# Residual tokens of x loaded in the steady slots of a perceiver block, into the place of the turned outputs

## The reference

```python
x = x + xattn(layernorm(x), ctx)      # softmax(q k^T / 8) v, heads joined, @ Wo + bo
x = x + attn(layernorm(x))            # note: attn adds its own (normalised) input too
x = x + ffn(layernorm(x))             # relu(x @ w1.T + b1), rounded, @ w2.T + b2, rounded
```

## Time and profile before

| what | us |
|---|---|
| median of 3 runs | 953.22 (950.82 to 953.23) |
| profiled execution | 953.45, span 951.7 |
| PE busy | 928.4 (98% of the span) |
| ACT, DVE, POOL busy | 584.0, 545.4, 493.5 |

### The profile page before, as it was taken

The page is one execution under the profiler, slowest core; times in us unless marked ns, Lnnn a source line. Parts: engine busy times, 40 slices in busy tenths (PEclk is TensorE's granted clock), DMA queues, the critical chain, the costliest instruction groups (busy, mean ns, idle before and its releaser), DMA issues.

```text
span 951.7 us, 19392 instructions
## 1 busy us (share of the span) xinstructions
PE 928.4 (98%) x7405; PEld 577.3 (61%) x7408; DVE 545.4 (57%) x980; ACT 584.0 (61%) x1095; POOL 493.5 (52%) x379
## 2 busy tenths in 40 slices
PE   5999999999999999999999999999999899999998
PEld 3556666666666666666666666666665445444443
DVE  7546555565556655565556655557667625375533
ACT  4577777777777777777777777777774122122220
POOL 3356665655666665655666665657778651110000
PEclk9999999999999999999999999999999899999999
DMA  8266677865766767676767667779978121212312
GB/s 298 67 169 133 132 135 153 147 145 124 143 137 131 139 138 157 137 145 131 134 136 143 134 131 151 131 143 146 166 157 167 56 55 43 48 43 93 96 34 78
DMA packets 313211, 120.05 MB, mean 126 GB/s; under 512 B 289952, under 2 KB 289952, under 8 KB 313120
## 3 DMA queue, kind: packets, MB, share of 16 engines
q1 hardware_dynamic: 298128, 89.97, 50.0%
q10 hardware_dynamic: 14992, 28.84, 9.4%
HBM read 45.36 MB, written 2.10 MB: 50 GB/s over the span
## 4 chain that ended last, share of the span: by engine, by line
PE 91%; DVE 4%; POOL 2%; ACT 1%; DMA 1%; issue 1%; POOLq 0%; DVEq 0%; ACTq 0%
PE v_ps L414 27%; PE k_ps L414 26%; PE e_ps L414 15%; PE e_ps L455 9%; PE o_ps L477 6%; PE o_ps L480 3%; PE o_ps L642 3%; PE v_ps L607 1%; PE o_ps L616 1%; DVE stats L946 1%; DVE xt_l L975 1%; DMA raw<-in_ctx_t 0%; DVE wv_l L964 0%; DMA x_in<-in_x 0%; POOL xr L1299 0%
## 5 line engine op out<-in xcount | busy, mean ns | idle before, releaser
L1271 POOL TENSOR_TENSOR p_l<-p_f,p_h 128x1024 f16<-128x1024 f32 x128 | 272.6, 2130 | 239.2 <-ACT p_f L784 238.3
L782 ACT ACTIVATE p_h<-e_ps,bias 128x512 f16<-128x512 f32 x256 | 175.9, 687 | 4.5 <-POOL p_l L1271 2.4
L784 ACT ACTIVATE p_f<-e_ps,bias 128x512 f32<-128x512 f32 x256 | 176.7, 690 | 0.0
L995 DVE TENSOR_TENSOR k_l<-k_ps,k_h 128x512 f16<-128x512 f32 x128 | 88.6, 692 | 145.6 <-ACT k_h L756 145.6
L987 DVE TENSOR_TENSOR v<-v_ps,v 128x512 f16<-128x512 f32 x128 | 88.9, 694 | 121.6 <-ACT v L748 121.6
L1000 DVE TENSOR_REDUCE q_max<-e_ps 128x2 f32<-128x1024 f32 x128 | 150.8, 1220 | 8.2 <-PE e_ps L455 0.2
L414 PE MATMUL v_ps<-wv_h,ctx_h 128*128 128x256 f16 x768 | 126.3, 273 | 0.8 <-DVE v L987 0.8
L414 PE MATMUL v_ps<-wv_l,ctx_h 128*128 128x256 f16 x768 | 125.7, 273 | 0.0
L414 PE MATMUL v_ps<-wv_h,ctx_l 128*128 128x256 f16 x768 | 125.7, 273 | 0.0
L1263 POOL TENSOR_TENSOR ctx_l<-raw,ctx_h 128x1536 f16<-128x1536 f32 x32 | 99.2, 3101 | 22.0 <-ACT ctx_h L737 21.3
L477 PE MATMUL o_ps<-v,pt_h 128*128 128x130 f16 x1024 | 106.0, 220 | 1.4 <-issue 1.4
(11 more groups left out here) (167 smaller groups left out, 1255.6 us busy)
## 6 DMA issues: line engine op xcount, KB each, us to landing
raw<-in_ctx_t ACTq DMA_DIRECT2D x26, 768.0 KB, 5.2
w_raw<-in_w_t SPq DMA_DIRECT2D x32, 256.0 KB, 2.8
raw<-in_ctx_t SPq DMA_DIRECT2D x6, 768.0 KB, 4.7
pt_h<-p_h SPq DMA_TRANSPOSE x128, 3.5
pt_l<-p_l SPq DMA_TRANSPOSE x128, 3.2
xr<-in_x ACTq DMA_DIRECT2D x8, 256.0 KB, 3.7
out<-xr SPq DMA_DIRECT2D x8, 256.0 KB, 2.0
x_in<-in_x ACTq DMA_DIRECT2D x6, 256.0 KB, 9.3
```

The source lines that it names most:

```text
L782: act.activation(p_h[:, s % H_RING, h, :], e_ps[s % 2][:, h, :], ACT.Exp, scale=EXP_SCALE, bias=bias[:, n % 2, h, q:q + 1]).then_inc(p_hi, 1)
L784: act.activation(p_f[:, s % F_RING, h, :], e_ps[s % 2][:, h, :], ACT.Exp, scale=EXP_SCALE, bias=bias[:, n % 2, h, q:q + 1]).then_inc(p_ful ...
L995: dve.tensor_tensor(k_l[:, n % 2, cols], k_ps[:, :], k_h[:, n % 2, cols], ALU.subtract).then_inc(k_split, 1)
L1271: pool.tensor_tensor(p_l[:, s % L_RING, :, :], p_f[:, s % F_RING, :, :], p_h[:, s % H_RING, :, :], ALU.subtract).then_inc(p_split, 1)
```

## The change

The tokens of x are loaded in slots 100 to 107. Rows 6 and 7 go to `xr`, rows 0 to 5 into rows 0 to 5 of `o_all`, once the turned output of that batch has landed. POOL adds the bias there in slots 104 to 110. The bias steps leave the seam; `residual` reads x from its new home (`x_home`) and waits for all eight biases. POOL's `o_norm(30)` goes ahead of `p_low(126)`, its inverse deviations follow each other. DVE's `norm(4)` and `norm(5)` go behind the `turned_low` steps. `project(19)` goes ahead of `project(22)`. The four `w2_round` of block 0 move from steps 0, 2, 4, 6 to steps 3 to 6. POOL's wait for the small loads moves ahead of its slots.

```diff
+        LOAD_X = {100: 6, 101: 7, 102: 0, 103: 1, 104: 2, 105: 3, 106: 4, 107: 5}
+        ADD_BIAS = {104: (6, 7, 0), 106: (1,), 108: (2, 3, 4), 110: (5,)}
+        def x_home(r):
+            return o_all[:, r, :] if r < 6 else xr[:, r, :]
-        made = list(range(19)) + [20, 21, 22, 19, 23]
+        made = list(range(19)) + [20, 21, 19, 22, 23]
...
+            project(19)
             project(22)
-            project(19)
             logits(1)
...
-            def load_x(r, after):
-                if after:
-                    act.wait_ge(wx_split, after)
-                act.dma_start(xr[:, r, :], x[r]).then_inc(xr_landed[r], 16)
+            def load_x(r):
+                if r < 6:
+                    act.wait_ge(ot_landed[r], 32)
+                act.dma_start(x_home(r), x[r]).then_inc(xr_landed[r], 16)
...
-                if s == SLOTS - 4:
-                    load_x(6, 0)
-                    load_x(7, 0)
-                ...
+                if s in LOAD_X:
+                    load_x(LOAD_X[s])
...
-                dve.wait_ge(xb_ready, r + 1)
-                dve.scalar_tensor_tensor(xr[:, r, :], out_bank(r), 1.0 / (W_SCALE * W_SCALE), xr[:, r, :],
+                dve.wait_ge(xb_ready, B)
+                dve.scalar_tensor_tensor(xr[:, r, :], out_bank(r), 1.0 / (W_SCALE * W_SCALE), x_home(r),
...
-                    if j % 2 == 0:
+                    if block == 0 and 3 <= j < 7:
+                        w2_round(0, j - 3)
+                    elif block and j % 2 == 0:
                         w2_round(block, j // 2)
...
             residual(5)
-            norm(4)
             turned_low(1, 0)
             turned_low(1, 1)
+            norm(4)
             residual(6)
-            norm(5)
             turned_low(1, 2)
             turned_low(1, 3)
+            norm(5)
...
+                for r in ADD_BIAS.get(s, ()):
+                    add_bias(r)
...
-            pool.wait_ge(small_landed, 96)
             p_low(SLOTS - 3)
-            add_bias(0)
-            add_bias(1)
+            o_norm(STAGES - 2)
             p_low(SLOTS - 2)
             p_low(SLOTS - 1)
-            ...
+            for r in range(3):
+                inverse_deviation(r)
             o_norm(STAGES - 1)
-            ...
+            for r in range(3, B):
+                inverse_deviation(r)
```

More of the change, by code:

```diff
@@ L901, in hidden_round @@
                                scale=1.0 / W1_SCALE, saturate=False).then_inc(h_q8, 1)
[L903 to L907, removed]
+            for s in range(SLOTS, SLOTS + X_LAG):
+                steady(s)
             turned_high(1, 0)
@@ L1298, in add_bias @@
                 pool.wait_ge(xr_landed[r], 16)
-                pool.tensor_tensor(xr[:, r, :], xr[:, r, :], bo_row[:, :], ALU.add).then_inc(xb_ready, 1)
+                pool.tensor_tensor(x_home(r), x_home(r), bo_row[:, :], ALU.add).then_inc(xb_ready, 1)
             def inverse_deviation(i):
@@ L1304, in inverse_deviation @@
                 inverse_root(mean_var[:, r, 1:2], rstd[:, r:r + 1], exponent[:, 0:1], len(x_groups) + i)
+            pool.wait_ge(small_landed, 96)
             def weight_high(i):
@@ L1330, in add_norm @@
                 pool.tensor_tensor(xr[:, r, :], xr[:, r, :], o_all[:, r, :], ALU.add).then_inc(x1n_ready, 1)
-            pool.wait_ge(small_landed, 96)
             p_low(SLOTS - 3)
-            add_bias(0)
-            add_bias(1)
+            o_norm(STAGES - 2)
             p_low(SLOTS - 2)
             p_low(SLOTS - 1)
[L1338 to L1343, removed]
-            o_norm(STAGES - 1)
[L1345 to L1350, removed]
+            for r in range(3):
+                inverse_deviation(r)
+            o_norm(STAGES - 1)
+            for r in range(3, B):
+                inverse_deviation(r)
             def norm_low(what, r):
```

## The result

The changed kernel takes 945.72 us (median of 6 runs, 944.99 to 946.1) where the kernel before takes 953.23 (6 runs, 950.82 to 953.6). The ratio is 0.9927, with a 95% interval of 0.9917 to 0.9938: between 5.9 and 7.9 us are won, 7.5 by the medians. The forecast was 945.3, with a range of 943.8 to 948.6. The profiled execution of after took 946.05 us; its span is 944.2, where the one of before had 951.7.

The account below looks back on a forecast made before the run. The prediction took PE to bound the kernel, so only its waits could be won: 0.6 + 5.96 + 0.78 + 0.70 = 8.04 us off the profiled 953.45 left 945.4, forecast as 945.3, range 943.8 to 948.6.

Parts of the forecast that it names:

- term 1: Seam, `weighted_values(124)` to `weighted_values(127)`: without x loads the transpose lands earlier; 0.6 us won, bounds 0 to 1.38.
- term 2: Seam, `turn(1, 2)` to `project(0)`: without bias steps PE's hole and the slow clock go; 5.96 us, bounds 3.0 to 5.96.
- term 3: At `logits(1)`: `project(22)` in between hides ACT's copy of `project(19)`; 0.78 us won, bounds 0 to 0.78.
- term 4: Ahead of `turn(2, 6)`: without `w2_round(0, 0)` ahead of `turned_low(2, 4)` PE's wait goes; 0.70 us, bounds 0 to 0.70.
- steady slots: Slots 100 to 110: added loads and biases cost 0, between 0 and 1 us; a late `pt_l` has 5.2 us slack.
- clock part: Seam, behind PE's hole: turns and matmuls at clock 0.50 cost 2.99 us, forecast to be won whole.
- its own range: Range of the forecast without rivals: 944.0 (late transposes' gain whole) to 947.5 (a `turned_low` late by 1 to 2 us).
- Rival 1: Seam: the holes go but the clock falls all the same; price 2.99 us, 948.3 us, chance 0.10.
- Rival 2: Seam: the change doesn't free PE's bank, hole and slow clock stay; 951.1 us, chance 0.05.
- Rival 3: Steady slots: eight loads hold up transposes, each costing PE 1.38 us, 11.0 in all; 956.2 us, chance 0.04.

Follow-up runs that it names:

- e2: The changed kernel with `o_norm(30)` moved on POOL from ahead of `p_low(126)` to behind `inverse_deviation(1)`; 945.15 us, ratio 0.9912.
- c1: The kernel before, unchanged, profiled a second time; 953.83 us.
- e5: The changed kernel with the loads of x rows 5, 6 and 7 back at the seam, their bias steps where POOL is idle; 946.71 us, ratio 0.9932.
- e4: The changed kernel with all eight bias steps and POOL's old order back in the seam, the loads left in the steady slots; 948.80 us, ratio 0.9967.
- e1: The kernel before with one exchange on POOL, `add_bias(4)` ahead of `o_norm(31)`; 950.96 us, ratio 0.9976.
- e8: The kernel before with only POOL's and DVE's orders in the seam changed, loads and biases left there; 949.86 us, ratio 0.9974.
- e3: The kernel before with only `project(19)` ahead of `project(22)` and the four `w2_round` of block 0 in steps 3 to 6; 950.83 us, ratio 0.9976.
- e6: The changed kernel with all eight x loads issued in slot 104 and the biases in slots 108 to 111; 950.24 us, ratio 0.9980.
- e9: The changed kernel with two x loads in each of slots 104 to 107 and the biases in slots 108 to 111; 946.74 us, ratio 0.9943.
- e7: The changed kernel with DVE's order undone, `norm(4)` and `norm(5)` again ahead of the `turned_low` steps; 945.59 us, ratio 0.9931.
- c2: The kernel before, unchanged, profiled a third time; 952.89 us.

## Why the prediction was right, step by step

| | predicted us | measured us, profile against profile |
|---|---|---|
| term 1, late transposes | 0.6 | 14.12 - 13.41 = 0.71 |
| term 2, bias steps in the seam | 5.96 | 32.89 - 26.20 - 0.71 = 5.98 |
| term 3, order of the keys | 0.78 | 67.75 - 66.81 = 0.94 |
| term 4, rounding of w2 | 0.70 | 19.79 - 18.89 = 0.90 |
| steady slots and start | 0 | -1.06 |
| sum | 8.04 | 7.47 (spans: 951.7 - 944.2 = 7.5) |

**What bounds it.** Right. PE had no wait from 80 to 721 us before or after, and all of the gain came from the places where it waited.

**Term 1: the size was right, one of its reasons wrong.** The chain came out as worked out: `weighted_values(124)` starts 727.52 - 723.38 = 4.14 us after `project_out(0)` before, and 2.60 after; of these 1.5 us 0.7 are left at `weighted_values(127)`, where the new wait of 0.58 us stands (0.8 forecast). But the prediction put the 0.6 us on POOL's order, with `o_norm(30)` ahead of `p_low(126)` ("if the order on POOL wins nothing" was its bound of 0), and called the transposes behind it bound by POOL and SP, with no x load near. That order wins nothing. In before POOL was free 0.69 us before it began `p_low(126)`, and it didn't wait for ACT, which the row names: by the starts ACT's steps stand at the same places in before and in e2, and in e2 `p_low(126)` begins at 2.81 us. It waited for the slow `pt_l(124)`, whose source it overwrites (`p_low(s)` waits in the code for the transpose of slot s - 2), as the rows of c1 and e5 name it. That one landed at 721.65 + 5.8 = 727.45, and POOL began at 727.87. So the loads held up POOL too. e4 moves them and leaves POOL's order alone, and has the whole term: 14.12 - 13.33 = 0.79 us, for 0.71 in after. The new order exchanged two bias steps (2.49 us) for `o_norm(30)` and its own wait, which left `p_low(126)` where it was (3.85 for 3.72), and e2 shows the 0.94 us that it could have won. The chain was right for this order; why before was slower, and the order beside it, were not worked out.

**Term 2: right in mechanism, half of it a draw of one execution.** Each link came within 0.2 us: `project(0)` was forecast for 749.7, and 750.64 less the 1.06 us by which the seam began later is 749.58; the spare time at `turn(1, 2)` was forecast as 1.1 us and is 1.05, at `project(0)` 0.5 and 0.45. e4 shows the cause, since putting the bias steps and POOL's old order back brings back DVE's 3.17 us, the hole and the slow clock; e1 and e8 show that orders alone win 1.6 and 2.6 us. Of the 5.96 us the hole's 2.97 are certain: four executions have it at 2.7 to 2.9. The 2.99 for the clock are what the one profile showed, and the largest of four: the mean is 1.7. By that mean term 2 is worth 4.7 us. The Trainium skill (TensorE: Matmul & The Clock Gate, Part 1) holds that the full rate has to be earned by recent activity. The traces agree, but don't make it a price: behind the same hole before shows 0.50 and e3 kept 1.00. The runs without a profile say the same: of the 52 of the kernel before that were taken beside the experiments, 14 have a mean granted clock of 1.00, and they took 951.4 us in the mean, the other 38 952.9 (where in the run their clock fell is not recorded).

**Terms 3 and 4: right, and 0.16 and 0.20 us too small.** e3 shows them alone. They were taken from the idle brackets (0.78, 0.70), and the starts moved by 0.94 and 0.90. The matmuls' ends are modelled, and the bracket begins at the modelled end; the true gap was longer. The same is seen at `weighted_values(124)`: 1.38 in the bracket, 1.54 by the starts.

**The steady slots: 0 as forecast, with less room than was claimed.** Slack of 5.2 us was set against 2.6 us for a load (a row with three loads of x beside it). One load of x added 1.7 us to a transpose that stood beside a context load, and together they made it 7.2 - 3.2 = 4.0 us late, which leaves 1.2. Where the weights are loaded the 5.2 us are used up without any x load (8.4 - 3.2), so nothing shows room for an x load there. And a second path was costed at nothing: each issue holds ACT's queue (0.33 to 0.51 us each in after, 0.65 in the row of six). e6 shows what happens past the edge on both paths. Two loads in a slot (e9) are not shown to cost anything in their slots; one in a slot is the safe side of an edge that lies between two and eight.

**The sum.** By the starts the four terms come to 8.53 us. 1.06 us of it are gone by a later start of the seam in this execution. It arose ahead of 80 us (80.00 for 78.92), where of all edits only POOL's moved wait for the small loads lies; and c1, which doesn't have that edit, is 1.42 us late at the same place (80.34), and e7, which has it, is not late at all (78.92). So nothing speaks for a cost of the change. Set against the medians, the account is 8.5 less 1.3 for a clock part above its mean, 7.2 us, beside the 7.0 us of the ratio. So the forecast of 945.3 was within 0.4 us partly by luck: a clock part 1.3 us too large met terms 1, 3 and 4, 0.5 us too small, and an execution of before that stood 0.8 to 1.2 us above the medians of its later runs (952.2 to 952.6). The lower end of its own range, 944.0 for "term 1 whole", doesn't come out of its terms: 0.78 us more than forecast give 944.5. Nothing hangs on it.

**The rivals.** Rival 1 (the clock falls with no hole) didn't come: no slice from 722 to 762 us of the profiles of after, e1, e2, e5, e7, e8 and e9 shows a clock under 1.00, and their longest hole there is 1.90 us (e5). Rival 2 (the bank is not freed) didn't come; e1 shows its first half, a hole of 1.77 us that order alone leaves. Rival 3 is real with eight loads crowded into a slot (e6); with one in a slot it didn't come.

## What to carry to other kernels

When a step moves from a seam where the bounding engine waits into a stretch where it never does, its price there is set by how many of them fall together, on the DMA engines and on the queue that issues them: spread them out, keep clear of the places where other loads use the slack up, and look at the slowest transfer, not at the median. Where the profile names an engine as what ended a wait and that engine had long been done, look for a DMA. A clock drop behind a hole should go into the sum as a mean over several executions, with the hole alone as the certain part. And where a hand-written order is changed, work out the neighbouring order too: e2, 0.9 us shorter in the seam, was one move away from the change.

## What was not expected of the hardware

- The same hole of 2.7 to 2.9 us on PE was followed by a granted clock of 0.50 in three executions, which took 2.99, 1.86 and 1.67 us more than the work, and by 1.00 in a fourth (0.25 us more). Behind holes of 2.09 (e4) and 2.64 us (e6) the clock fell to 0.50, behind 1.77 (e1) and 1.90 us (e5) it didn't.
- A `norm` on DVE (128x512 float32, SBUF to SBUF, 0.52 us alone) took 1.48 and 1.61 us when a POOL addition of the same size ran beside it, which itself took its usual 1.26 to 1.27 us. `residual`, with one operand in PSUM, took 0.68 us beside an addition as well (750.18 in before, the addition from 749.76 to 751.03). The Trainium skill (SBUF — State Buffer, SBUF: two separate sides) describes an exclusive lock on a port pair of the two engines, held for a whole instruction. The traces agree: in each of 22 places where a `norm` ran into an addition that was under way, or began 0.06 us after it (profiles of before, c1, c2, e1, e3, e4, e5 and e8, 720 to 760 us), the `norm` ended 0.27 to 0.29 us after the addition, whether it took 0.69 or 1.61 us itself. In the one place where the `norm` was ahead by 0.15 us it kept its time, and the addition took 1.53 us for 1.27 (e4):

```profile
748.55 0.54 DVE L1094 TENSOR_SCALAR o_all<-xr,mean_var,rstd 128x512 f32<-128x512 f32 x1
...
748.70 1.53 POOL L1297 TENSOR_TENSOR xr<-xr,bo_row 128x512 f32<-128x512 f32 x1
```

- A transpose of 128x1024 float16 lands in 3.2 us in the median, in 5.5 to 6.3 us beside three x loads of 256 KB (seven profiles), in 5.5 beside a context load, in 7.2 beside that and one x load, and in 12.4 beside eight x loads.
